# Two attentions' planes on their way through DRAM: stored once per plane and repeated by the loads, instead of stored once per use

## The chip, the cores and the metric

The kernel runs on one core of a Trainium2 chip. The metric is the device time of one execution in microseconds (us), the median of several runs. A core has five engines with queues of their own (TensorE, here PE with its weight loads PEld; VectorE, DVE; ScalarE, ACT; GpSimd, POOL; SyncE, SP) and 16 DMA engines. In this kernel every transfer is issued by SP, which works through its list in order: a wait in that list holds up all transfers behind it.

## What is computed

Eight images of 128 channels and 64x64 points go through two layers.

```python
# layer 0, per image: ll is a 32x32 half-resolution image (N0 = 1024 points), 8 heads of 16 channels
q = _l2norm(q); k = _l2norm(k)
attn = clip(einsum('bhnd,bhmd->bhnm', q, k) * scale)   # 1024 x 1024 per head
_, idx = top_k(attn, N // 2)                            # the larger half of each row is kept
out = softmax(masked attn) @ v                          # then proj, group norm
...                                                     # convolution branch, inverse wavelet, FFN
# layer 1, per image: N1 = 4096 points, one head of R = 16 channels
attn = softmax(einsum('bnr,brm->bnm', q, k) * scale)    # 4096 x 4096
out = gamma * (Wo @ (v @ attn)) + x
```

Both score matrices are products of 16-channel vectors. To get nearly float32 scores from bf16 matmuls, each of q and k is split into three bf16 **planes** (the value, the rest, the rest of the rest: planes 0, 1 and 2), and the score is the sum of six products of planes, listed in `TERMS`. The six products are stacked: q planes and k planes are laid on 6 x 16 = 96 partitions, so that one matmul of 96 rows gives the sum. So plane 0 of q stands in three 16-row blocks, plane 1 in two, plane 2 in one, and the same for k in another order.

## The kernel before, in words

The program handles image n's layer 0 beside image n-1's layer 1. Each image has a stage `between(f, n, fin, opn)`, in which the last part of image f = n-1's layer 0 (`fin`) and the opening of image n's layer 0 (`opn`) run together, and then a stage `slots`, one slot per head of layer 0 and per 512-row chunk of layer 1. There are nine `between` stages: the first has `opn` alone, seven have both, the last has `fin` alone. In every list the order is written out by hand; semaphores tie the engines together.

**Layer 0's planes** are made in `between`: `part0` on ACT (L1518, planes 0 and 1) and DVE (L2406 the rests, L2409 plane 2), each in two halves, q and k; semaphores `p0`, `p1`, `p2`. They lie in `PT`, channels on partitions. SP's `store_planes` writes them to the DRAM buffer `scr0`, which has the stacked layout `[q or k, head, term, 16, 1024]`: 12 stores of 256 KB per image, since every plane is stored once for each of its blocks. Then SP waits for all 12 (`scrw`), and `load_head` fetches a head with two loads (q and k, 96 rows of 2 KB each) into one of three places of `QK0`; heads 0 to 2 are fetched in `between`, heads 3 to 7 in the slots, three slots ahead. PE's `score0` (L446 in `products`) waits for head 0's semaphore `hq0` and stands ahead of `values1` (L990) in PE's list.

**Layer 1's planes** are made a little later in `between`: ACT L1475 (plane 0), DVE L2368, ACT L1478 (plane 1), DVE L2371 (plane 2); semaphores `p10`, `p11`, `p12`. `PT1` holds 4 quarters of the 4096 points x 32 rows (16 of q, 16 of k) on 128 partitions. SP waits for `p12`, stores the three planes to `scr1` (L406), waits for them (`scrw1`), and issues 12 loads of 128 KB (L410), one for each 16-row block of `QP1` and `KP1`. PE's `first()` begins with `maxima(0, 0)` (L548), which waits for all 12 (`qp1`). `first()` is a run of 32 matmuls whose row maxima DVE takes (L1928, `MX`), with four `update`s of layer 0's threshold search between them (L1701). Behind the 12 loads SP issues the 2 MB store of x (`scrX`, L413), and then the stores `scrL`.

One more transfer is looked at below, which the change leaves alone: in `load_done` (L300) the row sums of 7 heads are loaded onto 112 rows of `OB`, each head's row of 4 KB 16 times. Its source has the dimensions 7 x 16 x 1024, its destination 112 x 1024.

Of the kernel before, what the change touches and what calls it, by code (L numbers as in the profile page):

```python
# [7 lines left out]
N1 = H * W  # L8
# [9 lines left out]
TERMS = [(0, 0), (0, 1), (1, 0), (1, 1), (0, 2), (2, 0)]  # L18
# [80 lines left out]
def dwt_attention_kernel(nc, x, qkvT, projT, dw, pwT, w1T, w2T, qk1T, wv, woT, vec, cst, cstT, out,  # L99
# [4 lines left out]
    with ctx:  # L104
# [6 lines left out]
        scr0 = nc.dram_tensor("scr0", [2, NH, len(TERMS), HD, N0], bf16, kind="Internal").ap()  # L111
        scr1 = nc.dram_tensor("scr1", [3, 128, N0], bf16, kind="Internal").ap()
# [140 lines left out]
        def kp(h):  # L253
# [4 lines left out]
          scrw1 qp1 v1p v1c m mr mp mt mpt mq st1 e1 pv1 on nt xr0 xr1 y1 out0 out1 dset dimg dpr pimg g1 g2 g3 g4  # L258
# [6 lines left out]
        def _(sp):  # L265
# [10 lines left out]
            def load_head(h):  # L276
                done = s["hq%d" % (h % 3)]
                for w in range(2):
                    sp.dma_start(QK0[0:KS, h % 3, w, :], scr0[w, h].rearrange("j d n -> (j d) n")).then_inc(done, 16)

            def store_planes(n, t, made):
                sp.wait_ge(s[made], (n + 1) * 2)
                for j, pair in enumerate(TERMS):
                    for w in range(2):
                        if pair[w] == t:
                            sp.dma_start(scr0[w, :, j, :, :], PT[:, t, w * N0:w * N0 + N0]).then_inc(s["scrw"], 16)
# [148 lines left out]
            for i in range(3):  # L435
                sp.wait_ge(s["hq%d" % i], images * len(range(i, NH, 3)) * 32)
# [4 lines left out]
        def _(pe):  # L441
# [8 lines left out]
            def slots(b, l0, l1):  # L450
# [8 lines left out]
                def score(h, i):  # L459
# [12 lines left out]
                    if i == 0:  # L472
                        pe.wait_ge(s["hq%d" % (h % 3)], (b * len(range(h % 3, NH, 3)) + h // 3 + 1) * 32)
# [55 lines left out]
                def maxima(c, k):  # L529
# [10 lines left out]
                    if k == 0 and c == 0:  # L540
                        pe.wait_ge(s["qp1"], b * 192)
                        pe.wait_ge(s["v1c"], b * 8)
# [334 lines left out]
                for h in range(-1, NH):  # L877
# [8 lines left out]
                    if h < NH:  # L886
                        weigh(h - 1, 3)
                    if h < NH:
                        weigh(h - 1, 4)
                    if h < NH:  # L890
                        weigh(h - 1, 5)
# [3 lines left out]
                    if h < NH:  # L895
                        weigh(h - 1, 6)
                    if h >= 0:
                        maxima(h + 1, 0)
                    score(h + 1, 1)
                    if h < NH:  # L900
                        weigh(h - 1, 7)
# [3 lines left out]
            def between(f, n, fin, opn):  # L905

                def score0(i):
                    if not (fin and opn):
                        return
                    if i >= 1:  # L910
                        pe.wait_ge(s["eva"], (n * NH) * NT + i)
                    else:
                        pe.wait_ge(s["f2c"], f * 8 + 6)
                        pe.wait_ge(s["kon"], n + 1)
                        pe.wait_ge(s["hq0"], (n * len(range(0, NH, 3)) + 1) * 32)
# [255 lines left out]
        def _(act):  # L1171
# [14 lines left out]
            def slots(b, l0, l1):  # L1186
# [8 lines left out]
                def evict(h, i):  # L1195
# [4 lines left out]
                    if h == 1 and i == 0:  # L1200
                        need(act, s["scrw1"], b * 48)
# [462 lines left out]
        def _(dve):  # L1664
# [8 lines left out]
            def slots(b, l0, l1):  # L1673
# [325 lines left out]
                def search(h):  # L1999
                    if h >= 1:  # L2000
                        maxima(h, 24)
                    half_m(h - 1, 3, 0)
                    if h >= 1:
                        maxima(h, 25)
                    apart(h, 1)
                    half_m(h - 1, 3, 1)
                    if h >= 1:
                        maxima(h, 26)
                    half_m(h - 1, 4, 0)
                    if h >= 1:  # L2010
                        maxima(h, 27)
# [3 lines left out]
                    if h >= 1:  # L2015
                        maxima(h, 28)
                    half_m(h - 1, 5, 0)
                    if h >= 1:
                        maxima(h, 29)
# [721 lines left out]
```

## Time and profile before

| what | value |
|---|---|
| median of 3 runs | 5668.78 us (5662.02 to 5674.28) |
| profiled execution: span | 5667.7 us |
| its own time | listed only among the three runs above |
| PE busy | 4766.2 us (84%) |
| DVE busy | 4618.9 us (81%) |
| ACT busy | 4256.4 us (75%) |
| DMA, SP's queue | 104280 packets, 193.56 MB, 11.1% of 16 engines' span |

The span goes from the first to the last instruction. Busy shares are averages over stages with different limits. The share of the DMA engines is a mean over the 16: a transfer that runs on half of them can show at most 0.5.

### The profile page before, as it was taken

To read this page: it belongs to the slowest core of one execution; us is meant where nothing else is said; L and a number is where in the kernel's file an instruction comes from. 1 tells how busy PE (TensorE), PEld (TensorE's weight loads), DVE (VectorE), ACT (ScalarE), POOL (GpSimd) and SP (SyncE) were. 2 spreads that over 40 slices of the span, in tenths; PEclk is the share of its full clock that TensorE was granted. 3 is DMA by queue.
4 is the path that set the end of the run, shared out by engine and by line. 5 is a ranking of instruction groups with operands and counts; after the bars stand their busy time and mean duration, and the time that the engine had idled before them with its cause. 6 is when DMAs were issued, how large, how long until landed. Compare 5 with 4: busy or idle time off the path is not lost.

```text
span 5667.7 us, 92692 instructions
## 1 busy us (share of the span) xinstructions
PE 4766.2 (84%) x30180; PEld 3123.3 (55%) x30180; DVE 4618.9 (81%) x9087; ACT 4256.4 (75%) x6779; POOL 250.6 (4%) x125
## 2 busy tenths in 40 slices
PE   4444899988999889988999889998899889997799
PEld 2001366654666456663666546664466636664588
DVE  4887799987999789986999879997799879996553
ACT  3883699948998499966999489884899669994333
POOL 2001000010000200010000100002000100000000
PEclk7555799998999989998999989999899989998899
DMA  1001200012001110012000120011100120001100
GB/s 68 7 11 50 74 15 16 15 56 76 16 20 43 59 43 18 16 61 74 15 15 13 58 76 16 20 43 50 51 16 18 59 75 15 15 13 43 36 12 16
DMA packets 104805, 199.97 MB, mean 35 GB/s; under 512 B 36632, under 2 KB 41656, under 8 KB 100184
## 3 DMA queue, kind: packets, MB, share of 16 engines
q1 hardware_dynamic: 104280, 193.56, 11.1%
q8 instruction: 257, 4.21, 0.3%
q14 instruction: 268, 2.20, 0.1%
HBM read 110.61 MB, written 82.05 MB: 34 GB/s over the span
## 4 chain that ended last, share of the span: by engine, by line
PE 41%; DVE 23%; ACT 15%; issue 14%; SPq 3%; DMA 3%; DVEq 0%; ACTq 0%; POOL 0%; POOLq 0%
PE PS L582 16%; ACT work L1183 7%; PE PS L548 5%; DVE M L1760 4%; DVE MX L1928 4%; PE PS L566 4%; ACT work L1243 3%; DVE work L1751 3%; PE PS L514 3%; PE PS L524 3%; DVE work L1743 2%; PE PS L1057 2%; ACT arena L1175 2%; DVE arena L1857 2%; DMA work<-TPT 1%
## 5 line engine op out<-in xcount | busy, mean ns | idle before, releaser
L582 PEld LDWEIGHTS PS<-V,work 128*128 128x128 f32 x16384 | 2106.7, 193 | 155.8 <-issue 7.0
L582 PE MATMUL PS<-V,work 128*128 128x129 f32 x16384 | 2125.2, 277 | 2.5 <-ACT work L1243 1.2
L1183 ACT ACTIVATE work<-arena,T 128x1024 bf16<-128x1024 f32 x1504 | 1725.8, 1150 | 22.7 <-DVE T L1671 18.8
L1928 DVE TENSOR_REDUCE MX<-PS 128x1 f32<-128x512 f32 x2048 | 1399.3, 687 | 249.6 <-PE PS L548 233.9
L1243 ACT ACTIVATE work<-PS 128x1024 f32<-128x1024 f32 x1024 | 1046.8, 1024 | 334.0 <-PE PS L566 332.3
L548 PE MATMUL PS<-KP,QP 96*128 96x512 bf16 x2048 | 845.5, 414 | 137.3 <-DVE MX L1928 95.3
L566 PE MATMUL PS<-QP,KP 99*128 99x512 bf16 x2048 | 624.6, 387 | 77.5 <-ACT work L1243 54.2
L1175 ACT ACTIVATE arena<-PS 128x1024 f32<-128x1024 f32 x512 | 523.2, 1022 | 216.7 <-PE PS L446 209.5
L1857 DVE SCALAR_TENSOR_TENSOR arena<-PS,work 128x512 f32<-128x512 f32 x896 | 606.2, 684 | 67.3 <-ACT work L1235 65.3
L1760 DVE MAX8 M<-work 128x8 f32<-128x512 f32 x1024 | 648.4, 682 | 1.0
L1235 ACT ACTIVATE work<-PS 128x512 f32<-128x512 f32 x896 | 530.8, 601 | 119.9 <-PE PS L514 116.1
L548 PEld LDWEIGHTS PS<-KP,QP 96*128 96x128 bf16 x2048 | 200.5, 98 | 543.8 <-DVE MX L1928 419.1
L446 PE MATMUL PS<-work 96*128 96x512 bf16 x1024 | 350.5, 428 | 175.2 <-ACT arena L1175 167.2
L514 PE MATMUL PS<-work 99*128 99x512 bf16 x896 | 337.3, 388 | 93.7 <-DVE arena L1857 54.2
L1743 DVE TENSOR_SCALAR work<-arena,T 128x1024 f32<-128x1024 f32 x512 | 378.4, 745 | 2.3
L1751 DVE TENSOR_SCALAR work<-work,FL 128x1024 uint32<-128x1024 uint32 x512 | 375.9, 747 | 1.0
L524 PE MATMUL PS<-arena,VT 128*17 128x256 f32 x4096 | 321.4, 411 | 10.0 <-DVE arena L1849 5.8
L566 PEld LDWEIGHTS PS<-QP,KP 99*128 99x128 bf16 x2048 | 185.0, 99 | 222.6 <-ACT work L1243 126.5
L1183 ACT ACTIVATION_READ_ACCUMULATOR work<-arena,T 128x1 f32 x1504 | 302.9, 201 | 0.0
L446 PEld LDWEIGHTS PS<-work 96*128 96x128 bf16 x1024 | 80.4, 102 | 329.9 <-ACT arena L1175 272.2
L514 PEld LDWEIGHTS PS<-work 99*128 99x128 bf16 x896 | 83.2, 98 | 222.1 <-DVE arena L1857 127.0
L2614 POOL TENSOR_TENSOR work<-work 128x1024 f32<-128x1024 f32 x8 | 22.5, 2814 | 3509.9 <-DMA work<-in_x 3509.9
(193 smaller groups left out, 4160.8 us busy)
## 6 DMA issues: line engine op xcount, KB each, us to landing
scr<-work SPq DMA_DIRECT2D x96, 256.0 KB
work<-scr SPq DMA_DIRECT2D x128, 192.0 KB, 2.8
work<-in_x SPq DMA_DIRECT2D x16, 1024.0 KB, 7.7
arena<-in_x SPq DMA_DIRECT2D x8, 2048.0 KB, 9.9
scrX<-arena SPq DMA_DIRECT2D x8, 2048.0 KB, 14.2
XR<-scrX SPq DMA_DIRECT2D x64, 256.0 KB, 2.8
out<-YO SPq DMA_DIRECT2D x64, 256.0 KB, 2.0
scrL<-work SPq DMA_DIRECT2D x24, 512.0 KB, 2.6
```

What stands on the lines that cost most here:

```text
L514: mm(PS[:, c, :], kp(h)[0:KA, 128 * mt:128 * mt + 128], qp(h)[0:KA, 512 * c:512 * c + 512], start=True, stop=True).then_inc(s["st" if c el ...
L548: mm(PS[:, maxbank(c, k, l0), :], QP1[0:KS, c * 512 + 128 * i:c * 512 + 128 * i + 128], KP1[0:KS, 512 * w:512 * w + 512], start=True, stop ...
L566: last = mm(PS[:, pairbanks(k, l0) + t, :], KP1[0:KA, 128 * mt:128 * mt + 128], QP1[0:KA, j * 512:j * 512 + 512], start=True, stop=True)
L582: last = mm(PS[:, 5 + i // 2, 136 * (i % 2):136 * (i % 2) + 129], P1[:, (16 * j + k) % 3, t, 128 * i:128 * i + 128], V1[:, mt, :], start=( ...
L1175: A(scores(h, i), bank2(0), ACT.Copy, scale=0.25, accum_out=SUM[:, h % 2, i:i + 1]).then_inc(s["eva"], 1)
L1183: A(junk[:, m % 2, :], scores(h, i), ACT.Sign, scale=-1.0, bias=T[:, h % 2, i:i + 1], accum_out=CA[:, h % 2, i:i + 1]).then_inc(s["ca"], 1)
L1235: A(JA[:, mt % 2, 512 * c:512 * c + 512], PS[:, c, :], ACT.Exp, scale=0.25).then_inc(s["e" if c else "eh"], 1)
L1243: A(P1[:, (16 * j + k) % 3, :, :].rearrange("p t n -> p (t n)"), PS[:, u:u + 2, :].rearrange("p a n -> p (a n)"), ACT.Exp, scale=0.25).the ...
L1751: cp.did(V.tensor_scalar(JDu[:, c, :], JDu[:, c, :], FL[:, h % 2, i:i + 1].bitcast(u32), None, ALU.bitwise_xor))
L1760: cp.did(V.max(M8[:, i, a, :], JD[:, c, 512 * a:512 * a + 512]))
L1857: V.scalar_tensor_tensor(scores(h, mt)[:, 512 * c:512 * c + 512], PS[:, c, :], 0.0, JA[:, mt % 2, 512 * c:512 * c + 512], ALU.is_ge, ALU.m ...
L1928: V.reduce_max(MX[:, c % 2, i, w:w + 1], PS[:, maxbank(c, k, l0), :], AX.X).then_inc(s["mr"], 1)
```

## The change

Layer 0: `scr0` becomes `[plane, 128, 2, 1024]`. Each plane is stored once, when it is made, with one 512 KB store of 128 rows of 4 KB: 3 stores for 12. The repeating is done by the loads: `load_head` has 7 loads for 2 (one for q plane 0 three times, one for k planes 0 and 1 together, and so on). For head 0 five of them are issued as soon as planes 0 and 1 are in DRAM; its plane 2 is copied from `PT` by two transfers within the chip's SBUF (`head0_late`). Layer 1: `scr1` becomes `[plane, 32, 4096]`; each plane is stored when it is made; 7 loads with rows of 8 KB for 12. `TERMS` is reordered, so that blocks that share a source are neighbours. The total that the loads bring is the same: 384 KB per head, 1.5 MB for layer 1.

```diff
-TERMS = [(0, 0), (0, 1), (1, 0), (1, 1), (0, 2), (2, 0)]
+TERMS = [(0, 0), (0, 1), (0, 2), (1, 0), (1, 1), (2, 0)]
...
-        scr0 = nc.dram_tensor("scr0", [2, NH, len(TERMS), HD, N0], bf16, kind="Internal").ap()
-        scr1 = nc.dram_tensor("scr1", [3, 128, N0], bf16, kind="Internal").ap()
+        scr0 = nc.dram_tensor("scr0", [3, 128, 2, N0], bf16, kind="Internal").ap()
+        scr1 = nc.dram_tensor("scr1", [3, 32, N1], bf16, kind="Internal").ap()
...
-            def load_head(h):
+            def load_head(h, parts=(0, 1, 2)):
                 done = s["hq%d" % (h % 3)]
-                for w in range(2):
-                    sp.dma_start(QK0[0:KS, h % 3, w, :], scr0[w, h].rearrange("j d n -> (j d) n")).then_inc(done, 16)
+                d = slice(HD * h, HD * h + HD)
+                q, k = QK0[0:KS, h % 3, 0, :], QK0[0:KS, h % 3, 1, :]
+                if 0 in parts:
+                    sp.dma_start(q[0:48], scr0[0, d, 0, :].unsqueeze(0).to_broadcast([3, HD, N0])).then_inc(done, 16)
+                    sp.dma_start(k[80:96], scr0[0, d, 1, :]).then_inc(done, 16)
+                if 1 in parts:
+                    sp.dma_start(k[0:32], scr0[0:2, d, 1, :]).then_inc(done, 16)
+                    sp.dma_start(k[48:80], scr0[0:2, d, 1, :]).then_inc(done, 16)
+                    sp.dma_start(q[48:80], scr0[1, d, 0, :].unsqueeze(0).to_broadcast([2, HD, N0])).then_inc(done, 16)
+                if 2 in parts:
+                    sp.dma_start(q[80:96], scr0[2, d, 0, :]).then_inc(done, 16)
+                    sp.dma_start(k[32:48], scr0[2, d, 1, :]).then_inc(done, 16)
 
-            def store_planes(n, t, made):
+            def store_plane(n, t, made):
                 sp.wait_ge(s[made], (n + 1) * 2)
-                for j, pair in enumerate(TERMS):
-                    for w in range(2):
-                        if pair[w] == t:
-                            sp.dma_start(scr0[w, :, j, :, :], PT[:, t, w * N0:w * N0 + N0]).then_inc(s["scrw"], 16)
+                sp.dma_start(scr0[t].rearrange("p w n -> p (w n)"), PT[:, t, :]).then_inc(s["scrw"], 16)
+
+            def head0_late():
+                for w, row in ((0, 80), (1, 32)):
+                    sp.dma_start(QK0[row:row + HD, 0, w, :], PT[0:HD, 2, w * N0:w * N0 + N0]).then_inc(s["hq0"], 16)
...
                 if opn:
-                    store_planes(n, 0, "p0")
-                    store_planes(n, 1, "p1")
-                    store_planes(n, 2, "p2")
+                    store_plane(n, 0, "p0")
+                    store_plane(n, 1, "p1")
                     sp.wait_ge(s["vt"], (n + 1) * 2)
                     sp.sem_inc(s["free"], 1)
-                    sp.wait_ge(s["scrw"], (n + 1) * 192)
-                    for h in range(3):
+                    sp.wait_ge(s["scrw"], n * 48 + 32)
+                    load_head(0, (0, 1))
+                    store_plane(n, 2, "p2")
+                    head0_late()
+                    sp.wait_ge(s["scrw"], (n + 1) * 48)
+                    for h in range(1, 3):
                         load_head(h)
                 if fin:
-                    sp.wait_ge(s["p12"], f + 1)
-                    for a in range(3):
-                        sp.dma_start(scr1[a], PT1[:, a, :]).then_inc(s["scrw1"], 16)
-                    sp.wait_ge(s["scrw1"], (f + 1) * 48)
-                    for j, (tq, tk) in enumerate(TERMS):
-                        for w, (t, dst) in enumerate(((tq, QP1), (tk, KP1))):
-                            sp.dma_start(dst[16 * j:16 * j + 16].rearrange("p (j n) -> p j n", j=4),
-                                         scr1[t].rearrange("(j s) n -> s j n", s=32)[16 * w:16 * w + 16]).then_inc(s["qp1"], 16)
+                    for a, made in enumerate(("p10", "p11", "p12")):
+                        sp.wait_ge(s[made], f + 1)
+                        sp.dma_start(scr1[a].rearrange("s (j n) -> j s n", j=4), PT1[:, a, :]).then_inc(s["scrw1" if a < 2 else "scry1"], 16)
+                    sp.wait_ge(s["scrw1"], (f + 1) * 32)
+                    planes = scr1.rearrange("t (w d) n -> t w d n", w=2)
+                    sp.dma_start(KP1[0:32], planes[0:2, 1]).then_inc(s["qp1"], 16)
+                    sp.dma_start(KP1[48:80], planes[0:2, 1]).then_inc(s["qp1"], 16)
+                    sp.dma_start(KP1[80:96], planes[0, 1]).then_inc(s["qp1"], 16)
+                    sp.dma_start(QP1[0:48], planes[0, 0].unsqueeze(0).to_broadcast([3, HD, N1])).then_inc(s["qp1"], 16)
+                    sp.dma_start(QP1[48:80], planes[1, 0].unsqueeze(0).to_broadcast([2, HD, N1])).then_inc(s["qp1"], 16)
+                    sp.wait_ge(s["scry1"], (f + 1) * 16)
+                    sp.dma_start(KP1[32:48], planes[2, 1]).then_inc(s["qp1"], 16)
+                    sp.dma_start(QP1[80:96], planes[2, 0]).then_inc(s["qp1"], 16)
```

The other edits follow from these: the counts in the waits on `hq0` to `hq2` (112 per head for 32) and `qp1` (112 per image for 192), and ACT's wait before it writes over the planes, which names `scry1` too. The lists of PE, DVE, ACT and POOL are the same; line numbers behind L286 shift.

On SP, in a `between` stage that has both parts, before the change: `work` is the buffer that holds `PT` and `QK0`, `scr` is scr0, and the numbers are the dimensions of the destination.

```order
L286 DMA scr<-work 8x16x1024 x12
L400 REGISTER_ALU
L279 DMA work<-scr 96x1024 x6
```

With the change, at the same place, up to the first of the two whole heads:

```order
L293 DMA scr<-work 128x2048 x2
L410 ISA
L281 DMA work<-scr 48x1x1024
L282 DMA work<-scr 16x1024
L284 DMA work<-scr 32x1x1024
L285 DMA work<-scr 32x1x1024
L286 DMA work<-scr 32x1x1024
L293 DMA scr<-work 128x2048
L297 DMA work<-work 16x1024 x2
```

Twelve stores and six loads became three stores, five loads, two transfers on the chip and, behind the rows shown, 14 loads for heads 1 and 2.

On SP, in the slots, two loads per head became seven at the same place:

```order
L281 DMA work<-scr 48x1x1024
L282 DMA work<-scr 16x1024
L284 DMA work<-scr 32x1x1024
L285 DMA work<-scr 32x1x1024
L286 DMA work<-scr 32x1x1024
L288 DMA work<-scr 16x1024
L289 DMA work<-scr 16x1024
L379 DMA work<-TPT 1x8x128 x3
```

Nothing else moved there: the rows of `TPT` still follow.

## Rows read from the trace of the kernel before

**Rows 1.** Waits, whole trace: who <- for whom: us in total, times, longest us.

```profile
PE PS L548 <- DMA KP<-scr: 13.1, 1, 13.1
PE PS L446 <- DMA work<-scr: 7.7, 6, 2.9
```

**Rows 2.** Chain that ended last, last image's stage: start us, us, what.

```profile
5269.07 1.24 DVE arena L2371
...
5271.18 2.54 DMA scr<-arena
...
5273.74 0.33 SPq L410
...
5278.80 9.69 DMA KP<-scr
```

**Rows 3.** Timeline of the third `between` stage: start us, us, engine, line, [idle before].

```profile
1290.92 13.92 SPq L286 DMA_DIRECT2D scr<-work  x12
1291.28 2.00 ACT L1518 ACTIVATE work<-work 128x1024 bf16<-128x1024 f32 x2
1300.77 1.21 DVE L2409 TENSOR_TENSOR work<-work 128x1024 bf16<-128x1024 f32 x1
1309.98 1.95 PE L976 MATMUL PS<-arena,w_qk 128*32 128x512 f32 x16
1313.17 1.06 ACT L1475 ACTIVATE arena<-arena 128x1024 bf16<-128x1024 f32 x1
1313.17 0.61 PE L446 MATMUL PS<-work 96*128 96x512 bf16 x2 [1.25 <-DMA work<-scr]
1338.21 0.59 PE L548 MATMUL PS<-KP,QP 96*128 96x512 bf16 x2 [0.47 <-ACT V L1484]
```

**Rows 4.** Timeline of PE, the fourth `between` stage.

```profile
1970.33 1.94 PE L976 MATMUL PS<-arena,w_qk 128*32 128x512 f32 x16
1975.20 1.03 PE L446 MATMUL PS<-work 96*128 96x512 bf16 x2 [2.93 <-DMA work<-scr]
2000.62 0.59 PE L548 MATMUL PS<-KP,QP 96*128 96x512 bf16 x2 [0.57 <-ACT V L1484]
```

**Rows 5.** Windows: engines' busy time, PEclk, DMA share of 16 engines, GB/s.

```profile
1297.00:1309.00 12.00, 9.91 (x25) 3.99 (x24) 10.12 (x22) 6.79 (x8) 3.19 (x2) 1.00 0.53 203
1311.00:1312.00 1.00, 0.93 (x12) 0.01 (x2) 0.00 (x0) 0.00 (x0) 0.00 (x0) 1.00 0.83 272
1327.00:1333.00 6.00, 2.36 (x15) 1.71 (x15) 0.00 (x0) 6.00 (x11) 0.00 (x0) 0.98 1.08 120
1337.00:1339.00 2.00, 1.33 (x8) 0.84 (x8) 1.03 (x5) 2.00 (x5) 0.00 (x0) 1.00 1.02 434
2532.00:2533.00 1.00, 1.00 (x10) 0.97 (x9) 0.58 (x2) 1.00 (x2) 1.00 (x2) 1.00 0.43 156
5177.20:5178.20 1.00, 1.00 (x8) 0.80 (x7) 0.58 (x2) 0.75 (x2) 0.00 (x0) 1.00 0.42 143
5179.20:5180.20 1.00, 1.00 (x10) 0.96 (x10) 0.00 (x0) 0.31 (x1) 0.00 (x0) 1.00 0.44 115
```

**Rows 6.** Timeline of SP, last image: the broadcast load that runs at 5177 to 5180.

```profile
5175.25 0.86 SPq L300 DMA_DIRECT2D arena<-scrD  x1
```

**Rows 7.** Groups by line in 1338.5 to 1364, the third stage's `first()`: xcount | busy us, mean ns.

```profile
L1928 DVE TENSOR_REDUCE MX<-PS 128x1 f32<-128x512 f32 x32 | 21.6, 691 | 0.7 <-PE PS L548 0.3
L1751 DVE TENSOR_SCALAR work<-work,FL 128x1024 uint32<-128x1024 uint32 x2 | 1.4, 750 | 0.0
```

**Rows 8.** Timelines, the first `between` stage (no layer 1 beside it).

```profile
104.98 1.01 PE L446 MATMUL PS<-work 96*128 96x512 bf16 x2 [0.16 <-DMA work<-scr]
108.86 1.00 ACT L1175 ACTIVATE arena<-PS 128x1024 f32<-128x1024 f32 x1
```

**Rows 9.** Timeline of SP, a slot of the third image.

```profile
1432.69 0.82 SPq L279 DMA_DIRECT2D work<-scr  x2
1465.74 2.02 SPq L368 DMA_DIRECT2D work<-TPT  x3
```

More of the change, by code:

```diff
@@ L257, in dwt_attention_kernel @@
           st e p pv o od rd odr ol oc pj fnd fsum dll cv pw x1 dgl f1 hc ge f2 f2c f2n x2 xs q1 q1c p10 r11 p11 p12
-          scrw1 qp1 v1p v1c m mr mp mt mpt mq st1 e1 pv1 on nt xr0 xr1 y1 out0 out1 dset dimg dpr pimg g1 g2 g3 g4
+          scrw1 scry1 qp1 v1p v1c m mr mp mt mpt mq st1 e1 pv1 on nt xr0 xr1 y1 out0 out1 dset dimg dpr pimg g1 g2 g3 g4
           g5 gs u1 u2 u3 u4 u5 hs qn ye si de dn bc bw xg xl sth eh ph dld dls kon dc1 dc2 free""".split()
@@ L435, in _ @@
             for i in range(3):
-                sp.wait_ge(s["hq%d" % i], images * len(range(i, NH, 3)) * 32)
+                sp.wait_ge(s["hq%d" % i], images * len(range(i, NH, 3)) * 112)
             sp.wait_ge(s["dls"], images * 48)
@@ L472, in score @@
                     if i == 0:
-                        pe.wait_ge(s["hq%d" % (h % 3)], (b * len(range(h % 3, NH, 3)) + h // 3 + 1) * 32)
+                        pe.wait_ge(s["hq%d" % (h % 3)], (b * len(range(h % 3, NH, 3)) + h // 3 + 1) * 112)
                     products(h, i)
@@ L540, in maxima @@
                     if k == 0 and c == 0:
-                        pe.wait_ge(s["qp1"], b * 192)
+                        pe.wait_ge(s["qp1"], b * 112)
                         pe.wait_ge(s["v1c"], b * 8)
@@ L885, in slots @@
                     l1_weigh(h - 1, 15, (1,))
[L886 to L891, printed above, removed]
+                    if h < NH: weigh(h - 1, 3)
+                    if h < NH: weigh(h - 1, 4)
+                    if h < NH: weigh(h - 1, 5)
                     score(h + 1, 0)
@@ L894, in slots @@
                     l1_score(h, 0)
[L895 to L898, printed above, removed]
+                    if h < NH: weigh(h - 1, 6)
+                    if h >= 0: maxima(h + 1, 0)
                     score(h + 1, 1)
-                    if h < NH:
-                        weigh(h - 1, 7)
+                    if h < NH: weigh(h - 1, 7)
                 closing()
@@ L914, in score0 @@
                         pe.wait_ge(s["kon"], n + 1)
-                        pe.wait_ge(s["hq0"], (n * len(range(0, NH, 3)) + 1) * 32)
+                        pe.wait_ge(s["hq0"], (n * len(range(0, NH, 3)) + 1) * 112)
                     products(0, i)
@@ L1200, in evict @@
                     if h == 1 and i == 0:
-                        need(act, s["scrw1"], b * 48)
+                        need(act, s["scrw1"], b * 32)
+                        need(act, s["scry1"], b * 16)
                         need(act, s["xs"], b * 16)
@@ L1999, in search @@
                 def search(h):
-                    if h >= 1:
-                        maxima(h, 24)
+                    if h >= 1: maxima(h, 24)
                     half_m(h - 1, 3, 0)
-                    if h >= 1:
-                        maxima(h, 25)
+                    if h >= 1: maxima(h, 25)
                     apart(h, 1)
                     half_m(h - 1, 3, 1)
-                    if h >= 1:
-                        maxima(h, 26)
+                    if h >= 1: maxima(h, 26)
                     half_m(h - 1, 4, 0)
-                    if h >= 1:
-                        maxima(h, 27)
+                    if h >= 1: maxima(h, 27)
                     half_m(h - 1, 4, 1)
@@ L2014, in search @@
                     excess(h, 0)
-                    if h >= 1:
-                        maxima(h, 28)
+                    if h >= 1: maxima(h, 28)
                     half_m(h - 1, 5, 0)
-                    if h >= 1:
-                        maxima(h, 29)
+                    if h >= 1: maxima(h, 29)
                     flip(h, 1)
```

## The prediction

> **What bounds the kernel now.** I read the waits first, for what DMA holds up. PE waits once for layer 1's planes, 13.1 us in the last image, and six times for head 0's planes, 7.7 us in all [rows 1]. All else that the change could give back lies under other work. The chain of waits shows the 13.1 us from within: plane 2 made at 5270.3, three stores, twelve loads issued from 5273.74 to 5279.2, the last landing at 5288.5 [rows 2]. In the seven images before it the same loads are hidden: in the third `between` stage PE begins `first()` at 1338.21 behind ACT, not behind a DMA [rows 3]. From there DVE is the bound: 32 row maxima at 691 ns fill 21.6 of 25.5 us with 0.7 us idle before them [rows 7], and layer 0's updates and passes stand between. So a late `qp1` moves all that follows by the same amount. The question is whether the new loads land before 1338.2.
>
> **How wide a transfer runs.** The windows tell more than the bytes [rows 5]. While the 12 old stores run (1297 to 1309), the DMA share is 0.53 at 203 GB/s. It stays there though the next store is already issued: two stores in flight use the same half of the engines. Their destination begins with a dimension of 8 (8 heads x 16 rows), their source with 128 rows: 8 of 16 engines, 25.4 GB/s each. The broadcast of L300 [rows 6] has a source that begins with 7, and runs at a share of 0.42 to 0.44, which is 7 of 16, with 143 to 156 GB/s at its best, 20 to 22 GB/s per engine, and 115 (16.4 each) at its worst. Transfers whose both sides begin with a multiple of 16 reach shares near 1: head loads of 96 rows 0.83 at 272 GB/s (20.5 each), the 2 MB store 434 GB/s (26.6 each). So I take it that **a transfer gets as many engines as the slowest dimensions of its two sides have in common, and that narrow transfers meet on the same engines**.
>
> The Trainium skill says this in "DMA: Bandwidth & Descriptors", section "Why a DMA increments its semaphore by 16 and not by 1": the largest k up to 16 that divides the slowest dimension, not of size 1, of both access patterns, on the lowest-numbered k engines. By that rule the trace agrees, and it speaks against this change. What it has beyond the rows is the lowest-numbered engines; were each narrow transfer on others, the sum would be that of the second rival.
>
> The new transfers begin so: `q[0:48]` and `QP1[0:48]` with 3 copies, `k[0:32]`, `k[48:80]`, `q[48:80]` and their like in layer 1 with 2 planes or copies, the stores to `scr1` with j = 4. Only the 16-row blocks and the new stores to `scr0` use all 16. The engine that serves every one of them, which I call engine 0, sets the pace. Four of a head's seven loads give it 32 KB each, 131 kB in all; layer 1's four wide loads 131 kB each, 524 kB, and with the three 16-row blocks 549 kB; each of the `scr1` stores 65.5 kB.
>
> **The parts, in the third `between` stage.**
> 1. *Head 0.* Plane 1 is made at 1293.3 [rows 3], its store lands near 1296. Five loads put 131 kB on engine 0, at 20 GB/s 6.6 us, until about 1303.5. Plane 2 is made at 1302.0 [rows 3]; its store and the two on-chip transfers land near 1306.3, before PE is through with L976 at 1311.9. The 1.25 us wait for head 0 goes. It was mostly free: from L976 to `first()` this stage took 28.2 us, the fourth, with a 2.93 us wait, 30.3 [rows 3, 4]. Gain 2.0 us, once. In the first image PE waited 0.16 us, and ACT took the result only at 108.86, 2.9 us behind PE: nothing [rows 8].
> 2. *Heads 1 and 2.* 14 loads from 1306.3 on; engine 0 gets 262 kB, 13.1 us at 20 GB/s, and is free at about 1320. The 14 issues at some 0.43 us [rows 2] take SP until 1312.5, before plane 0 of layer 1 is made at 1314.2 [rows 3].
> 3. *Stores to scr1.* 3 x 65.5 kB at 25.4 GB/s are 7.7 us behind that: 1327.7.
> 4. *Loads of layer 1.* Their issue waits for planes 0 and 1, near 1325, so they queue without a gap: 549 kB on engine 0. Their packets are of 8 KB. Between the 22 GB/s of 4 KB rows and the 26.6 of the big store I take 24: 22.9 us, to 1350.6, and 0.7 us to the semaphore: 1351.3. That is **13.1 us late**, in seven images: 91.7 us.
> 5. *Last image.* No heads in the way. Plane 1 is made near 5269.0 [rows 2]; its store starts on engine 0 near 5269.8, two stores of 2.6 us end at 5275.0, the loads at 5297.9, landing 5298.6 against 5288.5: 10.1 us more.
> 6. *The slots.* Seven issues of 0.43 us for two, 2.2 us more of SP, and 131 kB on engine 0, some 6.6 us. SP's next hurry, the rows of `TPT`, comes 33 us behind the load's issue [rows 9], and the head is wanted slots later. Nothing.
> 7. *Later in `between`.* The 2 MB store and `scrL` come behind the loads on engine 0, until about 1360; what waits for them comes after `first()`, which has moved too. Nothing.
>
> Sum: 91.7 + 10.1 - 2.0 = 99.8 us on the profiled span of 5667.7; that stands 1.1 us under the median of the runs, so 5768.6. I say 5768.
>
> **Bounds.** The rate of a few engines alone is not in the trace. With 26.6 GB/s throughout, the steady stage has heads until 1316.8, stores until 1324.2, loads until 1344.8: 7.1 us late; the last image 7.0: together +55 us, 5724. With the 16.4 GB/s of the worst broadcast window, 26.6 and 20.7: +205, 5874. I stand nearer the first, since 16.4 came in the tail of a transfer and larger packets go faster in the rows.
>
> **Rivals.**
> - *Narrow only in name: every transfer gets 16 engines.* Then layer 1's loads start at 5271.4 in the last image. At 120 GB/s, as the old ones ran [rows 5], 1.5 MB takes 13.1 us: 4 us gained, with step 1's 2.0 that is 5663. At the head loads' 272 GB/s it would be 11 and 2: 5656. For it: a program can be lowered in other ways than its code reads. Against: shares of 0.53 and 0.43 exactly where dimensions of 8 and 7 stand first. Chance 0.06.
> - *Narrow, but each on other engines.* Four wide loads would then take nine engines, 131 kB each, 5.5 us: landing near 1332, hidden under ACT as now, and near 5280.5 in the last image, 8 us gained; with the 2.0, 5659. This is the case that ends on the other side: it decides as soon as engine 0's queue is done before 1338.2. Against: two of the old stores together stayed at half the engines. Chance 0.06.
> - *Slow engines.* Rates of 18 GB/s and less when one engine reads and writes alone, +160 us and more, 5830 to 5874. For it: 115 GB/s over 7. Chance 0.13.
> - *SP is held.* The old stores took 1.16 us each to issue (13.92 / 12), as long as they took to move: SP is throttled when engines lag. If that held SP beyond the 33 us up to `TPT` in each slot it would cost more still; with 6.6 us of backlog per head it doesn't. Chance 0.02.
>
> **How the numbers follow.** The forecast, 5724 to 5830, has 0.73. A measurement of this kernel can tell 0.2%, 11.3 us, from no change. The first two rivals give 6 to 13 us less, mostly within that: of their 0.12 I give 0.03 to faster and 0.09 to same; slower has 0.88. The range leaves out the fast rivals and the end of the slow one: 5712 to 5845, its lower end a little under the bound, for packets of 8 KB on free engines.
>
> **What the profile will show.** In the windows behind L406 (1327 to 1344) a share of about 0.12 to 0.2 at 50 to 60 GB/s, for 1.08 at 120 before. PE L548 with a wait for `KP<-scr` or `QP<-scr` eight times, some 13 us each, for one. No wait of L446 for a DMA. Landing times of the wide layer 1 loads growing to 20 us and more. If those loads show a share near 1, or L548 waits in the last image alone, I am wrong from the root; if it waits eight times but for 5 or for 25 us, the rate was.

## The result, and the profile after

| | before | changed |
|---|---|---|
| median | 5665.4 us (5652.91 to 5674.28, 4 runs) | 5775.64 us (5767.94 to 5784.05, 4 runs) |
| profiled execution: span | 5667.7 us | 5766.1 us |
| ratio of the times | | 1.020, 95% interval 1.0179 to 1.0221 |

The forecast was 5768 us; the span was to grow by 99.8 us and grew by 98.4. The medians lie further apart, 110.2 us. The 12 us between the two numbers are mostly the choice of the execution: a run's time stands 1.8 us above its span, so the profiled execution of the changed kernel is its fastest run, 7.7 us under the median, and that of the kernel before stands some 4 us above its own.

The **waits** of the changed kernel, for PE's `first()` (L567, L548 before) and its weight loads. Columns: engine, what waits and its line, what it waits for, us in total, times, the longest.

```profile
PE PS L567 <- DMA QP<-scr: 114.7, 8, 27.3
PEld PS L567 <- DMA QP<-scr: 73.6, 6, 13.4
```

Before, this wait came once [rows 1]; now it comes eight times. Head 0's wait (L446 before, L465 now) is gone from the list. The **timeline of PE** in the third `between` stage shows both (start, us, engine, line, operation; in brackets the idle time and who ended it):

```profile
1319.07 2.27 PE L989 MATMUL PS<-arena,w_qk 128*32 128x512 f32 x16
1321.27 0.61 PE L465 MATMUL PS<-work 96*128 96x512 bf16 x2
...
1346.31 1.44 PE L959 MATMUL PS<-GGH,indT 32*128 32x2 f32 x6
1358.69 1.03 PE L567 MATMUL PS<-KP,QP 96*128 96x512 bf16 x2 [10.94 <-DMA QP<-scr]
1360.08 1.21 PE L567 MATMUL PS<-KP,QP 96*128 96x512 bf16 x2 [0.36 <-DVE MX L1942]
```

PE goes from the projection (L989) to head 0 (L465) without a gap. Then it stands still for 10.94 us before `first()`, where before it waited 0.47 us for ACT [rows 3]. The seven such waits ahead of the last image are 13.12, 10.94, 12.40, 13.32, 11.17, 12.16 and 14.32 us, together 87.4; the last is 27.27 against 13.08 before.

The **timeline of SP** in the same stage has the reason: the first and the last load of the two whole heads, then layer 1's three stores and its loads.

```profile
1314.04 0.75 SPq L281 DMA_DIRECT2D work<-scr  x1
...
1322.20 0.42 SPq L289 DMA_DIRECT2D work<-scr  x1
1323.69 4.11 SPq L420 DMA_DIRECT2D scr<-arena  x3
1333.14 0.66 SPq L423 DMA_DIRECT2D KP<-scr  x1
...
1336.84 0.42 SPq L430 DMA_DIRECT2D QP<-scr  x1
1337.55 0.38 SPq L432 DMA_DIRECT2D scrX<-arena  x1
```

The first store goes out as soon as plane 0 is made. The loads go out 9.4 us later, when planes 0 and 1 are in DRAM, and the last lands at 1358.6, 25.5 us after that. In the last image, where no heads are loaded, the **chain of waits** reads (start, us, what):

```profile
5352.03 1.24 DVE arena L2379
5353.26 0.02 issue
5353.28 9.97 DMA scr<-arena
5363.25 0.02 issue
5363.27 0.32 SPq L429
5363.59 0.05 issue
5363.63 22.01 DMA QP<-scr
5385.64 0.09 issue
5385.73 0.60 PE PS L567
```

Plane 2's store takes 9.97 us, against 2.54 for the last of three before [rows 2]: it stands behind the other two. The last load takes 22.01 us, against 9.69. The **windows** tell how wide these transfers run. Columns: stretch, its length, busy time of PE, PEld, DVE, ACT and POOL, granted clock, mean share of the 16 DMA engines, GB/s.

```profile
5353.00:5357.00 4.00, 4.00 (x36) 3.91 (x36) 0.25 (x1) 2.20 (x4) 0.00 (x0) 1.00 0.25 72
5357.00:5361.00 4.00, 1.46 (x14) 1.27 (x12) 0.00 (x0) 1.38 (x3) 0.00 (x0) 1.00 0.25 79
5373.00:5385.00 12.00, 0.00 (x0) 0.00 (x0) 0.00 (x0) 0.00 (x0) 0.00 (x0) 0.50 0.14 60
```

While the stores run, the share is 0.25, four engines of 16, and they move 72 to 79 GB/s, 18 to 20 each. In the last 12 us of the loads the share is 0.14, a little over two engines, at 60 GB/s, and most of the others have long been through. PE, DVE and ACT do nothing at all in these 12 us. PE's granted clock, 1.00 (2.4 GHz) while it worked, is 0.50 (1.2 GHz) in this stretch.

Two more rows of the page of the changed kernel: the sixth part (transfer, number, KB each, median us from issue to landing), and the fourth (the chain's share by engine).

```profile
scrX<-arena SPq DMA_DIRECT2D x8, 2048.0 KB, 26.0
...
PE 39%; DVE 22%; ACT 15%; issue 13%; DMA 7%; SPq 3%; POOL 0%; DVEq 0%; ACTq 0%; POOLq 0%
```

The 2 MB store `scrX` is as wide as the machine, and yet it lands 26.0 us after its issue, for 14.2 before: it ends only when the engines that serve the narrow loads have come to their part of it. The trace has a mark at the semaphore for each engine's part: in the last image, issued at 5364.1, 13 parts are through by 5371.5, one at 5376.5 and the last two at 5390.0 and 5390.5. Nobody waits for it there.

### The profile page after: what moved, and what is told of

Its sections match the earlier page's. It is cut to its first block, busy times and chain, and to the rows that moved or that the text cites. A ratio compares the mean times of both kernels' runs of the same rounds, so it can differ in the third digit from the quotient of the medians.

```text
span 5766.1 us, 92907 instructions
## 1 busy us (share of the span) xinstructions
PE 4775.6 (83%) x30180; PEld 3126.5 (54%) x30180; DVE 4613.5 (80%) x9087; ACT 4258.7 (74%) x6779; POOL 251.1 (4%) x125
## 4 chain that ended last, share of the span: by engine, by line
PE 39%; DVE 22%; ACT 15%; issue 13%; DMA 7%; SPq 3%; POOL 0%; DVEq 0%; ACTq 0%; POOLq 0%
PE PS L601 16%; ACT work L1196 7%; PE PS L567 5%; DVE M L1774 4%; DVE MX L1942 4%; ACT work L1257 4%; PE PS L585 4%; PE PS L533 3%; DVE work L1765 3%; DMA QP<-scr 3%; PE PS L543 3%; DVE work L1757 2%; DVE arena L1871 2%; PE PS L1070 2%; DMA work<-TPT 1%
## 5 line engine op out<-in xcount | busy, mean ns | idle before, releaser
L1257 ACT ACTIVATE work<-PS 128x1024 f32<-128x1024 f32 x1024 | 1046.8, 1024 | 335.0 <-PE PS L585 333.3
L567 PE MATMUL PS<-KP,QP 96*128 96x512 bf16 x2048 | 849.1, 416 | 231.8 <-DMA QP<-scr 114.7
L567 PEld LDWEIGHTS PS<-KP,QP 96*128 96x128 bf16 x2048 | 200.7, 98 | 640.7 <-DVE MX L1942 416.8
L465 PE MATMUL PS<-work 96*128 96x512 bf16 x1024 | 357.2, 435 | 164.3 <-ACT arena L1188 163.8
L465 PEld LDWEIGHTS PS<-work 96*128 96x128 bf16 x1024 | 82.0, 103 | 320.9 <-ACT arena L1188 270.1
```

The costliest lines, as they stand in the source:

```text
L567: mm(PS[:, maxbank(c, k, l0), :], QP1[0:KS, c * 512 + 128 * i:c * 512 + 128 * i + 128], KP1[0:KS, 512 * w:512 * w + 512], start=True, stop ...
L1257: A(P1[:, (16 * j + k) % 3, :, :].rearrange("p t n -> p (t n)"), PS[:, u:u + 2, :].rearrange("p a n -> p (a n)"), ACT.Exp, scale=0.25).the ...
```

## The experiments

The waits of PE for layer 1's planes, in each profiled execution, beside the medians. "Steady" is the mean of the seven stages with both parts, "extra" is their sum and what the last wait has over before's 13.1 us. "Narrow" is a transfer of which one side begins with 2, 3 or 4; "wide" is one over all 16 engines.

| run | heads' loads | layer 1's stores | layer 1's loads | steady, last (us) | extra (us) | median minus before's (us) |
|---|---|---|---|---|---|---|
| the change | narrow | narrow | narrow | 12.5, 27.3 | 101.6 | +110.2 |
| `l0_before` | wide | narrow | narrow | 11.3, 28.9 | 94.8 | +96.1 |
| `l1_store_pieces` | narrow | wide | narrow | 8.9, 22.9 | 72.0 | +81.0 |
| `l1_k_blocks` | narrow | narrow | QP1's narrow | 7.0, 23.8 | 60.0 | +69.9 |
| `l1_load_blocks` | narrow | narrow | wide | 1.5, 17.1 | 14.5 | +20.0 |
| `l1_before` | narrow | as before | as before | 0, 12.9 | -0.2 | +8.6 |
| `all_blocks` | wide | wide | wide | 0, 12.6 | -0.5 | -4.3 |
| `slots_narrow` | narrow in the slots | wide | wide | 0.1, 12.4 | 0.0 | +4.7 |
| `before_early` | as before | wide, early | wide, early | 0, 9.5 | -3.6 | -1.9 |
| `l1_merged` | as before | over 8 engines, early | wide, early | 0, 9.3 | -3.8 | -4.2 |
| `both_early` | wide | wide, early | wide, early | 0, 9.9 | -3.2 | -5.8 |

### Which layer: `l0_before` and `l1_before`

`l0_before` takes back layer 0 alone (12 stores, two loads per head), in the new order of `TERMS`:

```diff
-        scr0 = nc.dram_tensor("scr0", [3, 128, 2, N0], bf16, kind="Internal").ap()
+        scr0 = nc.dram_tensor("scr0", [2, NH, len(TERMS), HD, N0], bf16, kind="Internal").ap()
...
+                for w in range(2):
+                    sp.dma_start(QK0[0:KS, h % 3, w, :], scr0[w, h].rearrange("j d n -> (j d) n")).then_inc(done, 16)
```

> Layer 0's stores and loads as before, layer 1's as in the change. Theory N (narrow transfers share their first engines; layer 1's own transfers do the harm): the four wide loads of layer 1 keep the first engine 22 us, the waits of first() stay. If the stores to scr1 are as slow alone (60 GB/s on four engines in the last stage of the changed kernel) as in its last stage, each of eight waits stays within 2 us of the change's: +80 to +100 us against before, ratio 1.014 to 1.018, and head 0 waits again. Theory Q (step 2 of the prediction: the queue of heads 1 and 2 on the first engine holds the stores up, which themselves run at 25 GB/s per engine): waits of about 7.8 us for 12.5 in the seven stages, +55 to +70 us, ratio 1.010 to 1.012. Theory W (width does not matter, the later loads lose to layer 0's traffic): no wait left but the last, ratio 1.000.

Measured: 5761.86 us (ratio 1.016, 1.0144 to 1.0175). Layer 1's own transfers are the loss, nearly all of it. The waits for head 0 are back (seven, between 0.97 and 2.68 us), and the steady waits for layer 1 are 11.3 us for 12.5: without the 14 narrow loads of heads 1 and 2 ahead of them, layer 1's loads come hardly sooner. The stores say the same: from the first issue to the first load it takes 10.0 us here (1322.76 to 1332.79), 9.4 with the heads in the way. So the queue of heads 1 and 2 is not what the loss hangs on: theory Q, which had it hold up the stores, gave waits of 7.8 us.

`l1_before` takes back layer 1 alone:

```diff
-        scr1 = nc.dram_tensor("scr1", [3, 32, N1], bf16, kind="Internal").ap()
+        scr1 = nc.dram_tensor("scr1", [3, 128, N0], bf16, kind="Internal").ap()
...
+                    sp.wait_ge(s["p12"], f + 1)
+                    for a in range(3):
+                        sp.dma_start(scr1[a], PT1[:, a, :]).then_inc(s["scrw1"], 16)
+                    sp.wait_ge(s["scrw1"], (f + 1) * 48)
```

> Layer 1's stores and loads as before, layer 0's as in the change. Theory N: stores and loads of layer 1 run on all 16 engines behind the narrow loads of heads 1 and 2, which leave the first engine about 5 us after plane 2 of layer 1 is made; the last load lands about 2 us before or at the moment that PE comes to first(). Nearly all of the loss goes: -2 to +15 us against before, ratio 0.9995 to 1.003; PE waits for layer 1's loads some 13 us once, in the last stage. Rival H (the narrow loads of the heads do most of the harm): ratio above 1.010.

Measured: 5674.36 us (ratio 1.0017, 1.0006 to 1.0028): slower, by 8.6 us. PE waits for `KP<-scr` once, 12.9 us, as before. The waits for head 0, 7.7 us before, are gone here as in the change, and nothing was gained by it. The 8.6 us are taken up under `slots_narrow`.

### The width itself: `all_blocks`

Every load of the change in pieces of 16 rows, the stores to `scr1` in four pieces of 32 rows. Planes are still stored once each, the repeats are still the loads' affair, rows are still 8 KB, and SP has more to issue:

```diff
-                    sp.dma_start(q[0:48], scr0[0, d, 0, :].unsqueeze(0).to_broadcast([3, HD, N0])).then_inc(done, 16)
...
+                for t in parts:
+                    for j, pair in enumerate(TERMS):
+                        for w, dst in enumerate((q, k)):
+                            if pair[w] == t:
+                                sp.dma_start(dst[16 * j:16 * j + 16], scr0[t, d, w, :]).then_inc(done, 16)
...
+                        for j in range(4):
+                            sp.dma_start(scr1[a, :, N0 * j:N0 * j + N0], PT1[32 * j:32 * j + 32, a, :]).then_inc(s["scrw1" if a < 2 else "scry1"], 16)
```

> As the change, but every wide transfer is cut into pieces of 16 rows (the stores to scr1 of 32), so that each begins with a multiple of 16 on both sides: 12 loads per head and 12 for layer 1, each plane still stored once when made, same bytes, same rows of 2 and 8 KB. Theory N: the whole loss goes, and head 0's and the last stage's gains stay: -2 to -12 us against before, ratio 0.998 to 1.000; DMA share near 1 while the loads of layer 1 run. Rival R (it is the repeated reading of one row in DRAM, or the rows of 8 KB, that is slow): ratio stays above 1.010. Rival I (SP's 24 more issues per stage, 0.43 us each, make the stores of layer 1 late): +10 to +30 us, with layer 1's stores issued 2 us or more behind their planes.

Measured: 5661.49 us (ratio 0.9997, 0.9987 to 1.0007). The same bytes between the same places, and the whole loss is gone. So neither the once-stored planes nor the repeating loads cost anything that 0.1% would show; the first dimensions of 2, 3 and 4 do. By the Trainium skill, "DMA: Bandwidth & Descriptors", section "Why a DMA increments its semaphore by 16 and not by 1", a transfer uses as many engines, up to 16, as divide the slowest dimension (not of size 1) of both its sides, the lowest-numbered ones. The shares of 0.25 under the stores and 0.14 at the loads' end agree with the number of engines; that they are the lowest-numbered no run here shows, only that narrow transfers meet on the same ones.

### How much the stores cost: `l1_store_pieces`

The change, with only the store of the last diff in pieces.

> As the change, but each store to scr1 is cut into four of 32 rows, which run on all 16 engines. Theory N with slow narrow stores: from the making of plane 1 to the issue of the loads 4 us for 8.7 in the last stage; each of eight waits falls by 4 to 6 us: -32 to -48 us against the change, ratio to before 1.011 to 1.014. Theory Q: in the seven stages with heads the stores still stand behind the heads' loads, so only 1 to 3 us each: ratio 1.014 to 1.017. If the stores are not what is slow: ratio stays at 1.019.

Measured: 5746.8 us (ratio 1.0135, 1.012 to 1.015), 28.8 us less than the change. Here the first load goes out 7.2 us after the first store, for 9.4. Each wait is shorter by 3.6 us in the mean, the last by 4.4. The loads still take 26 us (issued at 1325.70, `first()` at 1352.08) and set the end.

### How much the loads cost: `l1_load_blocks` and `l1_k_blocks`

The first has all of layer 1's loads in 16-row blocks, the second only those of `KP1`:

```diff
-                    sp.dma_start(KP1[0:32], planes[0:2, 1]).then_inc(s["qp1"], 16)
-                    sp.dma_start(KP1[48:80], planes[0:2, 1]).then_inc(s["qp1"], 16)
+                    for row, t in ((0, 0), (16, 1), (48, 0), (64, 1)):
+                        sp.dma_start(KP1[row:row + 16], planes[t, 1]).then_inc(s["qp1"], 16)
```

> Layer 1's loads in twelve 16-row blocks, its stores still begin with a dimension of 4. Theory W (each engine works through its own queue; what a transfer puts on its busiest engine decides): the stores keep their 9.4 to 10 us, the loads take what the old ones took, 13.1 us at 120 GB/s. In the steady stages plane 0 is made 14.6 us before PE comes to first(); 10 us of stores, of which the last third runs under the first loads, and 13.1 us of loads end some 6 us behind the chip's own order, of which a little stays hidden: I expect waits of 4 to 7 us in seven images and 17 to 19 us in the last, 5695 to 5720. Rival (only the loads' width matters, the stores were always in time): no wait in the steady stages, 13 to 15 us in the last, 5662 to 5675.

> Only the two 32-row loads of KP1 become four 16-row blocks; those of QP1 stay 3 and 2 wide. Theory W with the bytes alone: engine 0 has 262 kB of wide loads and 57 kB of blocks for 549 kB, at 24.6 GB/s 13 us for 22.3; 9.3 us less, so steady waits of 3.2 us, the last 18.0: some 5700. Theory P (a 16-row block runs at 120 GB/s over all 16 engines, 7.5 GB/s on each, because its destination takes no more, so on engine 0 seven blocks cost 7.6 us and not 2.3): 10.7 + 7.6 us, 4 less than the change: steady waits of 8.5 us, the last 23: some 5743.

Measured: `l1_load_blocks` 5686.56 us (ratio 1.0043, 1.0028 to 1.0058). The steady waits shrink to 1.5 us, between the two expectations: I had put 4 to 7, and the time falls between them too. By the semaphores' marks in the trace the loads take 11.1 to 12.0 us behind the last store there, for the 13.1 I had taken. The last, 17.1 us, is where theory W had it. `l1_k_blocks` 5736.43 us (ratio 1.013, 1.0112 to 1.0147), waits of 7.0 and 23.8 us. Theory P had 5743 us with 8.5 and 23, the count of bytes alone 5700: the run is nearer P, with the steady waits between the two. The windows of the last image, first of `l1_load_blocks`, where next to nothing but 16-row blocks runs, then of `l1_k_blocks`, where the narrow loads of QP1 are left over at the end:

```profile
5285.00:5295.00 10.00, 0.00 (x0) 0.00 (x0) 0.00 (x0) 0.00 (x0) 0.00 (x0) 0.50 1.04 124
```

```profile
5331.00:5338.00 7.00, 0.00 (x0) 0.00 (x0) 0.00 (x0) 0.00 (x0) 0.00 (x0) 0.50 0.19 75
```

All 16 engines together move 124 GB/s into blocks of 16 partitions, 7.8 each. In the second window three engines move 75 GB/s, 25 each; of these bytes 38 packets of 8 KB are of the loads and 13 of 16 KB are of the 2 MB store behind them. An engine at a narrow load is thus three times as fast as one at a block. A 16-row block is not small change for engine 0: while all 16 engines are at it, it takes its share of a slow transfer. That is why replacing half of the bytes of the narrow loads by blocks gives back so little: behind the last store, engine 0's loads take 17.6 us in the mean of the steady stages for 23.1, and 19.0 for 22.4 in the last, where the bytes alone gave 9.3 us less.

### Something faster: `before_early`, `l1_merged` and `both_early`

`before_early` is the kernel before, with layer 1's planes stored when made and the ten loads of planes 0 and 1 ahead of plane 2:

```diff
-                    sp.wait_ge(s["p12"], f + 1)
-                    for a in range(3):
-                        sp.dma_start(scr1[a], PT1[:, a, :]).then_inc(s["scrw1"], 16)
-                    sp.wait_ge(s["scrw1"], (f + 1) * 48)
+                    for a, made in enumerate(("p10", "p11", "p12")):
+                        sp.wait_ge(s[made], f + 1)
+                        sp.dma_start(scr1[a], PT1[:, a, :]).then_inc(s["scrw1" if a < 2 else "scry1"], 16)
+                    sp.wait_ge(s["scrw1"], (f + 1) * 32)
```

> The kernel before, with layer 1's planes stored when made and the ten loads of planes 0 and 1 issued ahead of plane 2; all transfers as before, in width and number. Theory D (the twelve 16-row loads need 13.1 us at 120 GB/s, the destination's limit, and begin 1 to 2 us sooner): last wait 11 to 12 us for 13.1, 5663 to 5666, within 0.2% of before. Rival (the wait is mostly the stores and issues in front): last wait under 9 us, 5658 to 5661.

Measured: 5664.66 us (ratio 0.9995, 0.9986 to 1.0004). The last wait is 9.5 us for 13.1, between the two expectations. In `l1_merged` layer 0 is as before, and `scr1` gets a first dimension of 8 in which neighbouring planes are neighbouring rows, so that KP1 takes 32 rows in one load over all 16 engines:

```diff
+        scr1 = nc.dram_tensor("scr1", [8, 3, HD, N0], bf16, kind="Internal").ap()
...
+                        sp.dma_start(scr1[:, a], PT1[:, a, :]).then_inc(s["scrw1" if a < 2 else "scry1"], 16)
...
+                        src = scr1.rearrange("(j w) t d n -> w (t d) j n", w=2)[w, 16 * t:16 * u]
+                        sp.dma_start(dst[row:row + 16 * (u - t)].rearrange("p (j n) -> p j n", j=4), src).then_inc(s["qp1"], 16)
```

> Layer 0 as before. Layer 1's planes stored when made into a layout whose first dimension is 8 (half the engines), so that neighbouring planes are neighbouring rows: KP1 takes 32 + 32 rows with one dimension of 32 first (all 16 engines, 32 partitions at once), all else in 16-row blocks; ten loads for twelve. Theory D (a 16-row block is limited to 120 GB/s by its 16 partitions, a load over 32 partitions is not): the two 32-row loads take 1.1 us each instead of 2.2, the eight blocks 8.7 us: 10.9 us for 13.1; last wait 8 to 10 us, 5655 to 5664. Rival (120 GB/s is what rows of 2 KB into this tensor get, whatever the partitions): 13.1 us, last wait 11 to 13, 5663 to 5667. If waits show up in the steady stages, the stores over half the engines were too slow.

Measured: 5662.35 us (ratio 0.9994, 0.9983 to 1.0006), last wait 9.3 us. The windows over the loads of the last image, of `before_early` and then of `l1_merged`:

```profile
5273.00:5283.00 10.00, 2.44 (x21) 2.20 (x20) 0.00 (x0) 2.07 (x4) 0.00 (x0) 0.77 1.08 131
```

```profile
5268.00:5276.00 8.00, 0.77 (x7) 0.58 (x6) 0.00 (x0) 1.11 (x2) 0.00 (x0) 0.79 1.08 174
```

With the engines as busy (1.08), the loads of which a part spans 32 partitions bring 174 GB/s for 131. But the stores over half the engines were slower: the first load goes out 6.4 us after the first store, against 4.4 in `before_early`, and this used up the gain.

`both_early` puts the layer 0 of `all_blocks` and the layer 1 of `before_early` together.

> Layer 0 as in the version with all transfers over 16 engines (planes stored once, head 0's third plane on the chip), layer 1 as the kernel before but with each plane stored when made and the loads of planes 0 and 1 ahead of plane 2. If what these two give adds up: the six waits for head 0 are gone (7.7 us, of which 2 us at most count), the last wait is 9.5 us for 13.1 (measured alone): 3.6 to 6 us faster, 5660 to 5663, a ratio of 0.9990 to 0.9994. If the gains vanish among what the scheduler's slots take up, 5664 to 5668 with the same last wait of 9.5 us.

Measured: 5663.06 us (ratio 0.9991, 0.9981 to 1.0001), last wait 9.9 us. The ratio is where the gains add up, but its interval holds both cases. The last wait is shorter in all three, and their medians are 2 to 6 us below before's; none is shown to be faster, since each interval holds 1.

### The heads' loads in the slots: `slots_narrow`

In the table the runs with narrow head loads lie above their "extra", by 8.6 (the change), 9.0, 9.9, 5.5 and 8.8 us (`l1_before`); `l0_before`, `all_blocks`, `before_early`, `l1_merged` and `both_early`, whose head loads are wide, by 1.3, -3.8, 1.7, -0.4 and -2.6. This shows in medians alone. The spans of the profiled executions, from which the waits are, lie -7.8 to 11.9 us from their "extra" with narrow head loads and -9.8 to 7.3 with wide ones, since runs of one kernel differ by 15 to 25 us. To see where the 8 us come from, `all_blocks` got the change's narrow loads back for heads 3 to 7 alone:

```diff
+                if h >= 3:
+                    if 0 in parts:
+                        sp.dma_start(q[0:48], scr0[0, d, 0, :].unsqueeze(0).to_broadcast([3, HD, N0])).then_inc(done, 16)
...
+                    return
```

> The version with all transfers over 16 engines, but heads 3 to 7, which are loaded in the slots, by the change's seven loads with 3 and 2 in front; heads 0 to 2 and layer 1 stay wide. Theory S (the narrow head loads of the slots hold up the small transfers behind them on the same engines, above all the row of TPT, the store of YO and the load from scrD): YO lands 4.3 us after its issue and more, for 2.1; the waits for scrD are 20 us or more, for 16.8; those of PE for TPT 41 or more, for 37.8; the time 6 to 12 us above that version's 5661.5, so 5667 to 5674, near the one with layer 1 as before (5674.4). Rival (the 8 us come from heads 1 and 2 in the opening stage, or from how they shift it): YO lands late all the same, but scrD and TPT stay at 16.8 and 38 us and the time at 5659 to 5665.

Measured: 5668.13 us (ratio 1.0006, 0.9995 to 1.0017), 4.7 us over its before, where `all_blocks` is 4.3 under its own. The intervals of the two overlap by about half, and both hold 1, so the time doesn't settle it; the traces are plainer. From the waits (columns as above) and the page's sixth part, of `all_blocks` and then of `slots_narrow`:

```profile
DVE arena L2290 <- DMA arena<-scrD: 16.8, 8, 6.7
...
PE PS L528 <- DMA work<-TPT: 37.8, 49, 0.9
...
out<-YO SPq DMA_DIRECT2D x64, 256.0 KB, 2.1
```

```profile
DVE arena L2302 <- DMA arena<-scrD: 19.9, 8, 7.2
...
PE PS L540 <- DMA work<-TPT: 40.9, 49, 1.3
...
out<-YO SPq DMA_DIRECT2D x64, 256.0 KB, 4.8
```

Behind the narrow head loads the 256 KB store of `YO`, over all engines, lands 2.7 us later than behind the wide ones, and the two waits grow by 3.1 us each, 6.2 together: theory S's signs, with the two waits 0.1 us short of its figures. (The spans of the two, 5663.3 and 5657.4 us, are of one execution each and prove nothing.) The other profiled executions, before's among them, fall in the same two groups: `YO` lands in 4.3 to 4.8 us in the five with narrow head loads and in 2.0 to 2.1 in the six with wide ones; the waits for `scrD` are 20.3 to 21.6 and 14.3 to 16.8 us, those for `TPT` 40.9 to 43.5 and 37.8 to 40.0. So narrow head loads in the slots do delay what stands behind them; how much of the 8 us that is, and how much comes from heads 1 and 2, stays open.

## Why the prediction was right, and where its parts were off

**Width, and one engine for all narrow transfers: right.** The shares, the eight waits and `all_blocks` bear it out. The rivals that had every transfer over 16 engines, or each narrow one on engines of its own, foretold no wait in the steady stages. Slow engines, at 18 GB/s and less, are out for the loads, which ran at 23 to 24; the stores of the last image come near them.

**Step 1, head 0: the wait went, the 2.0 us can't be seen.** `l1_before` has that part and is 8.6 us slower, with the narrow head loads in it. `all_blocks` has it without them and stands 4.3 us under before, but its interval holds 1: a gain of 2.0 us is under what these runs can tell.

**Steps 2 to 4, the third stage: each term came out.** On the clock of the changed kernel this stage stands 9.4 us later (plane 0 of layer 1 made at 1323.7 for 1314.2). The marks at the semaphores in the trace tell when each term ended:

| | foretold, with 9.4 | measured | its length, foretold and measured |
|---|---|---|---|
| heads 1 and 2 through on engine 0 | 1329.4 | 1327.7 | 13.7, 13.7 |
| the three stores | 1337.1 | 1335.7 | 7.7, 8.0 |
| the loads | 1360.7 | 1358.6 | 23.6, 22.9 |

Over the seven stages the stores are through 7.4 to 8.7 us behind the heads, and the loads take 22.9 to 23.6 us behind the stores: 549 kB at 23 to 24 GB/s, for the 24 that were taken. The waits have 87.4 us for the 91.7. The heads' loads moved faster than the 20 GB/s per engine of step 2, 24.4 in this window (a share of 0.20 is 3.2 engines); that they ended no earlier fits their issue, which went on from 1314.0 to 1322.6, 0.6 us each in the mean for 0.43:

```profile
1317.00:1318.00 1.00, 1.00 (x2) 0.34 (x1) 0.46 (x1) 0.00 (x0) 0.00 (x0) 0.50 0.20 78
```

**What they leave out: the stores take as long with nothing ahead of them.** By steps 2 and 3 the stores would be done some 5 us earlier without the heads' queue. They are not. In the last image, where there are no heads, plane 0's store lands 6.5 us after its issue, plane 1's 3.5 us and plane 2's 3.6 us after the one before: 13.6 us from the first issue (5349.7 to 5363.25), for 12.0 in the third stage. In `l0_before`, third stage, where the last wide head load lands 2.0 us after the first store is issued, it is 12.7 us. Behind the narrow head loads of the third stage each store took 2.6 to 2.8 us on its four engines, 23 to 25 GB/s each, nearly as taken; in the last image, on engines with nothing else to do, 18 to 20 by the windows, and less in the first 3 us. Why, no run shows. So the right sum of the steady stages owes something to luck: the queue that it counts on hides a slowness that it doesn't know of. (The 25.4 GB/s of step 3 are also 203 GB/s over 8 engines; by the share, 0.53 or 8.5 engines, as the other rates were read, they are 23.9.)

**Step 5, the last image, +10.1: measured +14.2.** No queue hides the stores there. And I had two stores ahead of the loads on engine 0, where plane 2's store is a third. From plane 0 to the last landing the change takes 36.0 us (5349.6 to 5385.6), before took 21.8 (5266.7 to 5288.5). The stores end 5.3 us later than I had them, the loads behind them take 22.4 us for 23.6.

**Step 6, the slots, nothing: a term is missing.** I had compared the head loads with their own consumers and with the issue of `TPT`'s rows, 33 us behind. What else passes through engine 0 in between, the store of `YO`, the load from `scrD` and those rows, I left out; `slots_narrow` shows each of them held up. Its size is not settled: `l1_before`, with all head loads narrow, is 8.6 us over before (ratio 1.0006 to 1.0028), `slots_narrow` 4.7 us with an interval that holds 1.

**The bounds.** The upper one, said to be at 16.4 GB/s, leaves the stores at 25.4. At 16.4 they take 12.0 us and not 7.7, and the steady waits would be 30.9 us for 26.6. The range held at one value the term that came out worst in the last image.

## What to carry to other kernels

Before merging transfers, look at the first dimension of both sides: a broadcast of 3 or a pair of planes in front leaves 3 or 2 of 16 engines, and all such transfers queue on the same few. Count what a list of transfers puts on its busiest engine, not its bytes in all, and price a full-width transfer into few partitions by its time, not its bytes, when all engines come to it together. Look, too, at small transfers issued behind narrow ones. A mean share of DMA that looks idle (0.14) can be the bound.

## What the runs showed of the hardware

- Four engines wrote to DRAM at 18 to 20 GB/s each when nothing was ahead of them (last image), and at 23 to 25 each behind a queue of loads (2.6 to 2.8 us for 65.5 kB, third stage). Two to three engines read into 32 and 48 partitions at some 26 each (60 GB/s at a share of 0.14). Eight, in the kernel before, wrote 203 GB/s [rows 5].
- Loads into 16 partitions, over all 16 engines, one after the other, run at 124 to 131 GB/s, with rows of 2 KB (`before_early`, 131) and of 8 KB (`l1_load_blocks`, 124 over 5285 to 5295). With two of ten loads over 32 partitions the mean is 174. The Trainium skill, "SBUF — State Buffer", section "Door 1: The DMA port swizzle (why `[64,N]` ≈ `[32,N]`)", gives 16 partitions 4 of SBUF's 16 ports, some 109 GB/s, and 32 partitions twice as much. The order agrees; the runs lie above its figure, with several such loads in a row, into changing partitions, and not one alone.
- Transfers issued behind narrow ones use the engines that are free: after the narrow loads were issued, the share was 0.96 to 1.00 at 350 to 426 GB/s (5365 to 5369 and 1340 to 1344), most of it the 2 MB store, and its end still waited for the busy few.
